# Moving the first weights of stage 3, and their high and low parts, into the last group of stages 0-2

## The chip, the cores and the metric

The kernel runs on one core of one Trainium2 chip. The time is the device time of one execution in microseconds (us); lower is better. The engines are named as the profile names them: PE is TensorE, DVE is VectorE, ACT is ScalarE, POOL is GpSimd, SP is SyncE.

## What is computed

The reference is a chain of four blocks over 16 batch entries of 128 rows and 256 columns, all in float32, with a context of the same shape:

```python
x = _L0_xattn_ref(x, ctx, ...)          # attention over channels, context as keys and values
x = _L1_xattn_ref(x, ctx, masks, ...)   # self-attention, cross-attention to ctx, MLP (tanh gelu)
x = _L2_xattn_ref(ctx, x, mask, ...)    # "lat": latents x attend to ctx and x, rms norm, MLP
# stage 3: two cross-attentions to ctx, 16 heads of width 128, then an MLP (exact gelu)
res = x; h = _layer_norm(x, ln1_scale, ln1_offset)
x = res + _cross_attention(h, ctx, wq1, bq1, wk1, bk1, wv1, bv1, wo1, bo1, bias_k1, bias_v1)
...
```

## The kernel before

The kernel has two blocks. `stages_0_to_2` computes the first three reference blocks, `stage_3` the fourth. A block ends with a meeting of all engines; no instruction of stage 3 starts before all of the block before has ended.

**Stages 0-2.** The 16 batch entries are taken as 8 groups (g = 0 to 7) of two. Each group passes through a layer of steps, and the steps of neighbouring groups are interleaved by a plan: `SCORES`, `WORK`, `NORMS`, `ADDS` and `MASKS` hold a due time for each step, a group's steps are due 100 plan units after those of the group before, and the sorted lists `TENSOR_ORDER`, `VECTOR_ORDER`, `SCALAR_ORDER` and `GPSIMD_ORDER` are the programs of the engines. All engines work their lists in order. In the last group nothing of a later group fills the gaps. Its end is a chain: the last attention (`lat`) gives `lat_o`; VectorE adds the residual (`residual`, line 713) and takes its statistics; `norm("rms", 7)` turns them into a factor through 13 steps on 128x2 elements, each waiting for the one before (lines 737 to 763), and scales two 128x256 rows (line 747); TensorE transposes them (line 821), ScalarE copies them out (line 564), TensorE runs the eight ups (line 834), ScalarE the gelus (line 598), TensorE the downs (line 855), and VectorE adds the residual to `X`.

**Stage 3.** TensorE multiplies in the format fp32r, with each operand kept as a high part (HI, a rounded copy) and a low part (LO, the original minus the high part); a product is three passes (`PASSES`, `split_matmul`, line 1789). High parts are casts on ScalarE (`split_hi`, line 1376; `context_high`, line 1495), low parts subtracts on GpSimd (`split_lo`, line 1265; line 1277) or VectorE (`context_low`, line 1700). SyncE loads the raw weights of the next pair of heads (`load_qk`, `load_v`, `load_o`). The attention runs over 2 x 8 pairs of heads, the middle ones in a loop (`pair`). Before the first pair there is an opening, the section "open": ScalarE and VectorE make the parts of `ctxT` and of the first weights, VectorE computes the norm of all 16 rows of X in `norm_factors` (lines 1621 to 1638) and half of the normalised rows (`xhat_rows`, line 1643), ScalarE the other half. TensorE's order in the opening is keys 4 and 5, values 0 (24 matmuls), transposes of rows 0 and 1 (16, line 1800), keys 6, values 1 and so on, into four PSUM banks that are used in turn (`OPEN_WORK`); VectorE's `copy_k` (line 1567) and `copy_v` (line 1574) empty them.

## Time and profile before

| what | value |
| --- | --- |
| time, median of 3 runs (lowest to highest) | 2135.85 us (2134.97 to 2145.02) |
| the profiled execution's own time | 2138.81 us |
| its span, first to last instruction | 2136.7 us |
| mean granted TensorE clock, as a share of full speed | 0.973 |
| TensorE busy | 1941.6 us, 91% of the span |
| VectorE, ScalarE, GpSimd busy | 1275.5, 1187.1, 671.9 us (60%, 56%, 31%) |
| seam between the two blocks | about 957 us after the start |

Busy time is an average over stages with different limits: what a change in one place is worth is read from that place. Times in a timeline are microseconds from the start of the span. Where several equal instructions are merged (x4), the time is that of all. What stands in square brackets is the idle time of the engine before them and what ended it. The granted clock is 1 at 2.4 GHz and 0.5 at 1.2 GHz.

### The profile page before, as it was taken

The page shows a single profiled execution, that of the slowest core. Times are in us where ns is not written, and L with a number is a line of the kernel's source. Part 1 is how long each engine was busy: PE and PEld are TensorE (multiplying, and loading weights), DVE is VectorE, ACT ScalarE, POOL GpSimd, SP SyncE. Part 2 cuts the span into 40 slices and gives each one's busy share as a digit, 9 for nine tenths or more (in the row PEclk, how much of TensorE's full clock was granted, in tenths as well). Part 3 has the DMA queues.
Part 4 walks back from the last instruction along what each step waited for, and adds up shares of the span by engine and source line. Part 5 has one row for each costly group of instructions (what it writes and reads, how often), then busy time and mean ns, then how long its engine had stood idle before and what let it go on. Part 6 is the DMA issues. An engine that isn't in the chain of part 4 may idle for free.

```text
span 2136.7 us, 43190 instructions
## 1 busy us (share of the span) xinstructions
PE 1941.6 (91%) x14880; PEld 1683.4 (79%) x14880; DVE 1275.5 (60%) x4128; ACT 1187.1 (56%) x3882; POOL 671.9 (31%) x611
## 2 busy tenths in 40 slices
PE   4678899999999989868999999999899999999889
PEld 3457678787777777647899999998789999999778
DVE  3577797978787765426455555556555555555663
ACT  2367877878787777425444444444544444444531
POOL 1233444444444443214222221223321222122462
PEclk8799999999999999968999999999999999999999
DMA  6000000000000000001000000000000000000100
GB/s 258 8 9 7 6 12 2 12 4 4 4 4 4 2 1 1 1 16 44 21 25 25 20 15 25 17 23 26 10 26 16 25 25 20 15 20 0 40 11 30
DMA packets 24635, 44.35 MB, mean 21 GB/s; under 512 B 2336, under 2 KB 12064, under 8 KB 23584
## 3 DMA queue, kind: packets, MB, share of 16 engines
q1 hardware_dynamic: 23040, 33.67, 5.1%
q10 hardware_dynamic: 1440, 8.72, 1.0%
q8 instruction: 85, 1.39, 0.3%
q14 instruction: 70, 0.57, 0.1%
HBM read 40.28 MB, written 2.10 MB: 20 GB/s over the span
## 4 chain that ended last, share of the span: by engine, by line
PE 49%; DVE 3%; ACT 2%; issue 1%; POOL 1%; ACTq 0%; DVEq 0%
PE general L1789 33%; PE o_psum L1844 6%; PE scores L1828 5%; PE pT_psum L1903 3%; PE scores L1954 1%; ACT probs L1411 1%; DVE oT L1599 1%; ACT oT L1427 1%; PE o_psum L1954 1%; PE pT_psum L1954 1%; POOL probs L1314 0%; PE general L1800 0%; DVE guess L1625 0%; DVE qT L1643 0%; ACT kT L1394 0%
## 5 line engine op out<-in xcount | busy, mean ns | idle before, releaser
L489 POOL TENSOR_TENSOR probs<-probs,rsums 128x512 f32<-128x512 f32 (+1 forms) x288 | 282.7, 994 | 507.8 <-DVE rsums L691 507.1
L1314 POOL TENSOR_TENSOR probs<-probs,rsums 128x512 f32<-128x512 f32 x128 | 133.2, 1040 | 743.3 <-DVE rsums L1592 743.3
L525 ACT ACTIVATE probs<-negated,negmax 128x128 f32<-128x128 f32 (+1 forms) x768 | 325.4, 431 | 12.4 <-DVE negmax L682 12.1
L964 PE MATMUL pT_psum<-ident,probs 128*128 128x128 f32 x1088 | 179.4, 287 | 60.1 <-ACT probsT L533 29.0
L1419 ACT COPY probsT<-pT_psum 128x512 f32<-128x512 f32 x128 | 74.9, 585 | 286.2 <-PE pT_psum L1903 286.2
L964 PEld LDWEIGHTS pT_psum<-ident,probs 128*128 128x128 f32 x1088 | 126.9, 145 | 117.5 <-issue 65.7
L1789 PE MATMUL general<-ctxT,w_qk 128*128 128x512 f32 x768 | 201.4, 398 | 12.2 <-POOL w_qk L1265 7.0
L1789 PE MATMUL general<-hT,w_qk 128*128 128x512 f32 x768 | 205.9, 403 | 1.5 <-POOL hT L1283 0.8
L1789 PE MATMUL general<-w_o,oT 128*128 128x256 f32 x1536 | 192.7, 280 | 13.7 <-DVE oT L1599 13.7
L1789 PEld LDWEIGHTS general<-w_o,oT 128*128 128x128 f32 x1536 | 185.3, 188 | 22.6 <-DVE oT L1599 19.0
L1411 ACT ACTIVATE probs<-scores,negmax 128x128 f32<-128x128 f32 x512 | 180.1, 370 | 23.8 <-DVE negmax L1584 23.7
L1427 ACT ACTIVATE oT<-o_psum,hcols 128x512 fp32r<-128x512 f32 x128 | 88.0, 687 | 184.9 <-PE o_psum L1844 184.9
L1789 PEld LDWEIGHTS general<-w_v,ctxT 128*128 128x128 f32 x1536 | 185.0, 188 | 4.8
L1789 PE MATMUL general<-w_v,ctxT 128*128 128x256 f32 x1536 | 187.0, 278 | 0.0
L1789 PEld LDWEIGHTS general<-ctxT,w_qk 128*128 128x128 f32 x768 | 144.1, 190 | 43.8 <-POOL w_qk L1265 7.4
L697 DVE COPY probsT<-pT_psum 128x512 f32<-128x512 f32 (+1 forms) x144 | 93.9, 652 | 129.6 <-PE pT_psum L964 129.6
L1599 DVE SCALAR_TENSOR_TENSOR oT<-o_psum,hcols,oT 128x512 fp32r<-128x512 f32 x128 | 96.1, 751 | 122.3 <-ACT oT L1427 122.3
L1789 PEld LDWEIGHTS general<-hT,w_qk 128*128 128x128 f32 x768 | 136.2, 189 | 25.5 <-POOL hT L1283 1.0
L834 PE MATMUL general<-hT_y,weights_a 128*128 128x256 f32 x640 | 153.4, 386 | 2.8 <-ACT hT_y L564 1.9
L533 ACT COPY probsT<-pT_psum 128x512 f32<-128x512 f32 (+1 forms) x144 | 80.3, 558 | 131.1 <-PE pT_psum L964 127.7
L525 ACT ACTIVATION_READ_ACCUMULATOR probs<-negated,negmax 128x1 f32 x768 | 148.8, 194 | 0.0
L1844 PE MATMUL o_psum<-probsT,ctxT 128*128 128x128 f32 x1024 | 141.8, 281 | 1.4 <-ACT probsT L1419 1.4
(182 smaller groups left out, 3897.6 us busy)
## 6 DMA issues: line engine op xcount, KB each, us to landing
raw_qk<-w_qk_dram SPq DMA_DIRECT2D x32, 256.0 KB, 2.8
weights_a<-weights_a_dram ACTq DMA_DIRECT2D x2, 2048.0 KB, 18.1
raw_v<-w_v_dram SPq DMA_DIRECT2D x16, 256.0 KB, 2.7
raw_vrows<-vrows_dram SPq DMA_DIRECT2D x16, 256.0 KB, 3.4
raw_o<-w_o_dram SPq DMA_DIRECT2D x16, 256.0 KB, 2.6
weights_a<-weights_a_dram ACTq DMA_DIRECT2D x3, 1024.0 KB, 10.2
X<-x_dram SPq DMA_DIRECT2D x8, 256.0 KB, 7.7
ctx_in<-ctx_dram SPq DMA_DIRECT2D x8, 256.0 KB, 3.0
```

Of the source, the lines that this page charges most:

```text
L489: nc.gpsimd.tensor_tensor(pr, pr, rsums[:, n % 4, 0:segs].unsqueeze(2).broadcast_to([P, segs, width(kind) // segs]), ALU.mult).then_inc(s[ ...
L525: last = nc.scalar.activation(probs[:, n % PROBS, i * wide:(i + 1) * wide], src[:, i * wide:(i + 1) * wide], ACT.Exp, scale=1.0 if kind == ...
L697: nc.vector.tensor_copy(probsT[:, n % 4, 0:width(kind)], pT_psum[:, 0:width(kind)]).then_inc(s["pT_copied_dve"], 1)
L834: last = nc.tensor.matmul(out[:, j * RA:(j + 1) * RA], w[weight][:, c, chunk * P:(chunk + 1) * P], rhs(c), start=(c == 0), stop=(c == KC - 1))
L964: last = nc.tensor.transpose(pT_psum[:, j * P:(j + 1) * P], probs[:, n % PROBS, j * P:(j + 1) * P], ident[:, :])
L1314: nc.gpsimd.tensor_tensor(pr, pr, rsums[:, t % 2, :].unsqueeze(2).broadcast_to([P, NB, P]), ALU.mult).then_inc(s["probs_ready"], 1)
L1411: nc.scalar.activation(probs[:, t % 2, b * P:(b + 1) * P], scores[t % 2][:, b * P:(b + 1) * P], ACT.Exp, bias=negmax[:, t % 2, b:b + 1], s ...
L1427: nc.scalar.activation(oT[:, HI, head, quarter(t % G)], o_psum[:, :], ACT.Identity, bias=hcols[:, bass.ds(at, 1)]).then_inc(s["o_hi"], 1)
L1599: nc.vector.scalar_tensor_tensor(out=oT[:, LO, head, quarter(t % G)], in0=o_psum[:, :], scalar=hcols[:, bass.ds(at, 1)], in1=oT[:, HI, hea ...
L1789: last = nc.tensor.matmul(out, stationary(a, c), moving(b, c), start=(i == 0), stop=(i == len(terms) - 1))
L1828: last = nc.tensor.matmul(scores[t % 2][:, j * P:(j + 1) * P], qT[:, head, b * P:(b + 1) * P], kT[:, head, b * P:(b + 1) * P], start=True, ...
L1844: last = nc.tensor.matmul(o_psum[:, j * P:(j + 1) * P], v[:, head, (t % G) * NB + j, :], probsT[:, j * P:(j + 1) * P], start=True, stop=True)
```

## The change

The raw weights of the first pair of stage 3 (`w_qk` for both heads, `w_v`, `vrows`, `w_o`), `hcols` and `rows` are loaded by SyncE in the last group of stages 0-2, after the last down projection of `mlp1` has been made. ScalarE makes the high parts of `w_qk`, `w_v` and the whole of `ctxT` (seven casts) before it reads the `rms` transposes of group 7; GpSimd makes the low parts, and `vrow`, after its last add (three subtracts of 128x512, one of 128x256, four of 128x1024). VectorE makes no part of `ctxT` any more. The buffers, of which `early_parts` fixes the addresses before both blocks, lie over tensors of stages 0-2 that are dead by then; for that `WEIGHTS_A` and the order of the allocations are changed, so that the weights of `lat` and `mlp2`, which are still in use, lie elsewhere. The loads' order in stages 0-2 is the same. In stage 3 the corresponding loads, casts and subtracts and the waits on them are gone, and the semaphores are made before both blocks. The diff, cut to its core (the reordered allocations, the semaphore list and unchanged context are left out):

```diff
-WEIGHTS_A = [("wq0", 1, P), ("wk0", 1, P), ("wv0", 1, P),
+WEIGHTS_A = [("lat_q", KC, D), ("lat_k", KC, D), ("lat_v", KC, D), ("lat_o", KC, D),
+             ("mlp2_up", KC, F), ("mlp2_down", FC, D),
+             ("wq0", 1, P), ("wk0", 1, P), ("wv0", 1, P),
              ("self_q", KC, D), ("self_k", KC, D), ("self_v", KC, D), ("self_o", KC, D),
              ("cross_k", KC, D), ("cross_v", KC, D), ("cross_q", KC, D), ("cross_o", KC, D),
-             ("mlp1_up", KC, F), ("mlp1_down", FC, D),
-             ("lat_q", KC, D), ("lat_k", KC, D), ("lat_v", KC, D), ("lat_o", KC, D),
-             ("mlp2_up", KC, F), ("mlp2_down", FC, D)]
+             ("mlp1_up", KC, F), ("mlp1_down", FC, D)]
+LAST_WEIGHTS = sum(k * n for name, k, n in WEIGHTS_A if name.startswith(("lat", "mlp2")))
...
         READERS = {"ln1": ("self_q", "self_k", "self_v"), "ln2": ("cross_q",), "ln3": [f"mlp1_up{i}" for i in range(4)],
                    "lat": ("lat_q", "lat_k", "lat_v"), "rms": [f"mlp2_up{i}" for i in range(4)]}
         ROW_OF = {"self": 0, "cross": 1, "mlp1": 2, "lat": 3, "mlp2": 4}
+        late = early["s"]
+        def early_splits():
+            w_qk, raw_qk = early["w_qk"], early["raw_qk"]
+            yield "raw_qk0_loaded", 16, w_qk[:, 0, HI, :], w_qk[:, 0, LO, :], raw_qk[:, 0, :], "qk0_ready"
+            yield "raw_v_loaded", 32, early["w_v"][:, HI, :], early["w_v"][:, LO, :], early["raw_v"][:, :], "wv_ready"
+            yield "raw_qk1_loaded", 16, w_qk[:, 1, HI, :], w_qk[:, 1, LO, :], raw_qk[:, 1, :], "qk1_ready"
         with nc.Block() as block:
                     else:
                         load_mask_lat(g)
+                wait_made(sp, "mlp1_down", GA - 1)
+                for head in range(2):
+                    sp.dma_start(early["raw_qk"][:, head, :], dram["w_qk"][0, :, head, :]).then_inc(late[f"raw_qk{head}_loaded"], 16)
+                sp.dma_start(early["raw_v"][:, :], dram["w_v"][0, :, :]).then_inc(late["raw_v_loaded"], 16)
+                sp.dma_start(early["raw_vrows"][:, :, :].rearrange("p j n -> p (j n)"), dram["vrows"][0, :].partition_broadcast(P)).then_inc(late["raw_v_loaded"], 16)
+                sp.dma_start(early["raw_o"][:, :], dram["w_o"][0, :, :]).then_inc(late["raw_o_loaded"], 16)
+                sp.dma_start(early["hcols"][:, :], dram["hcols"]).then_inc(late["vectors_loaded"], 16)
+                sp.dma_start(early["rows"][:, :, :], dram["rows_b"].partition_broadcast(P)).then_inc(late["vectors_loaded"], 16)
+                sp.wait_ge(late["vectors_loaded"], 32)
             @block.gpsimd
             def _(pool):
                 nc.gpsimd.memset(v_self[:, :, :], 0.0).then_inc(s["v_zeroed"], 1)
                         cross_mask(g)
                     else:
                         lat_mask(g)
+                for i, (_, _, high, low, raw, ready) in enumerate(early_splits()):
+                    pool.wait_ge(late["hi_done"], i + 1)
+                    nc.gpsimd.tensor_tensor(low, raw, high, ALU.subtract).then_inc(late[ready], 1)
+                nc.gpsimd.tensor_tensor(early["vrow"][:, :], early["raw_vrows"][:, 0, :], early["raw_vrows"][:, 1, :], ALU.subtract).then_inc(late["vrow_ready"], 1)
+                for i in range(B // NB):
+                    at = slice(i * R, (i + 1) * R)
+                    pool.wait_ge(late["ctxT_hi"], i + 1)
+                    nc.gpsimd.tensor_tensor(early["ctxT"][:, LO, :, at], ctxT[:, :, at], early["ctxT"][:, HI, :, at], ALU.subtract)
             @block.scalar
             def _(act):
                     elif "_up" in name:
                         gelus(name[:4], int(name[-1]), g)
+                def early_high_parts():
+                    wait_made(act, "mlp1_down", GA - 1)
+                    for loaded, count, high, _, raw, _ in early_splits():
+                        act.wait_ge(late[loaded], count)
+                        nc.scalar.copy(high, raw).then_inc(late["hi_done"], 1)
+                    for i in range(B // NB):
+                        at = slice(i * R, (i + 1) * R)
+                        nc.scalar.copy(early["ctxT"][:, HI, :, at], ctxT[:, :, at]).then_inc(late["ctxT_hi"], 1)
                 for piece, kind, g, u in SCALAR_ORDER:
+                    if (piece, kind, g) == ("read", "rms", GA - 1):
+                        early_high_parts()
                     if piece == "exps":
                         exps(kind, g, u)
                     elif piece == "copy_act":
...
-def stage_3(nc, dram, consts):
+EARLY_BUFFERS = {"ctxT": ([P, 2, KC, B * P], F32R), "raw_qk": ([P, 2, 2 * KC * P], F32), "raw_v": ([P, KC * 2 * P], F32), "raw_o": ([P, 2 * D], F32),
+                 "raw_vrows": ([P, 2, 2 * P], F32), "w_qk": ([P, 2, 2, 2 * KC * P], F32R), "w_v": ([P, 2, KC * 2 * P], F32R), "w_o": ([P, 2, 2 * D], F32R),
+                 "vrow": ([P, 2 * P], F32), "hcols": ([P, 2 * NH * HCOLS], F32), "rows": ([P, len(ROWS_B), D], F32)}
+EARLY_BYTES = sum(4 * int(np.prod(shape[1:])) for shape, _ in EARLY_BUFFERS.values())
+def early_parts(nc, ctx):
+    early = {}
+    with ExitStack() as reserved:
+        reserved.enter_context(nc.sbuf_tensor("reserved", [P, LAST_WEIGHTS], F32))
+        for name, (shape, dt) in EARLY_BUFFERS.items():
+            early[name] = reserved.enter_context(nc.sbuf_tensor(name + "3", shape, dt))
+    early["s"] = {n: ctx.enter_context(nc.semaphore(n + "3")) for n in (
+            "raw_qk0_loaded", "raw_qk1_loaded", "raw_v_loaded", "raw_o_loaded", "raw_up_loaded", "raw_down_loaded",
...
             return ctx.enter_context(nc.semaphore(name))
         X = consts["X"]
+        s = early["s"]
+        kT = sb("kT3", [P, 2, B * P])
+        xhat_last = sb("xhat3", [P, 2 * NB, D])
+        sb("early3", [P, EARLY_BYTES // 4])
+        ctxT, raw_qk, raw_v, raw_o, raw_vrows = [early[name] for name in ("ctxT", "raw_qk", "raw_v", "raw_o", "raw_vrows")]
+        w_qk, w_v, w_o, vrow, hcols, rows = [early[name] for name in ("w_qk", "w_v", "w_o", "vrow", "hcols", "rows")]
         hT = sb("hT3", [P, 2, KC, B * P], F32R)
-        ctxT = sb("ctxT3", [P, 2, KC, B * P], F32R)
         qT = sb("qT3", [P, 2, B * P])
-        kT = sb("kT3", [P, 2, B * P])
         raw_ctxT = consts["ctxT"]
         v = raw_ctxT[:, :, :].rearrange("p c r -> p (c r)").rearrange("p (h b k) -> p h b k", h=2, b=B)
         oT = sb("oT3", [P, 2, 2, B * P], F32R)
...
                 def load_o(pair):
                     sp.dma_start(raw_o[:, :], dram["w_o"][bass.ds(pair, 1), :, :].rearrange("a p n -> p (a n)")).then_inc(s["raw_o_loaded"], 16)
-                load_qk(0, 0)
-                load_qk(0, 1)
-                load_v(0)
-                load_o(0)
                 def next_weights(pair, following):
...
                     pool.wait_ge(s["raw_v_loaded"], loads)
                     nc.gpsimd.tensor_tensor(vrow[:, :], raw_vrows[:, 0, :], raw_vrows[:, 1, :], ALU.subtract).then_inc(s["vrow_ready"], 1)
-                split_lo(qk_parts(0), raw_qk[:, 0, :], 1, "qk0_ready")
-                value_rows(32)
-                split_lo(v_parts, raw_v[:, :], 2, "wv_ready")
-                for g in range(G // 2, G):
-                    pool.wait_ge(s["ctxT_hi"], g + 1)
-                    nc.gpsimd.tensor_tensor(ctxT[:, LO, :, quarter(g)], raw_ctxT[:, :, quarter(g)], ctxT[:, HI, :, quarter(g)], ALU.subtract).then_inc(s["ctxT_late"], 1)
-                split_lo(qk_parts(1), raw_qk[:, 1, :], 3, "qk1_ready")
                 def split_h(a, g):
...
             @block.scalar
             def _(act):
                 seed(act, [s["exp_done"], s["pT_copied"], s["o_hi"], s["hi_done"], s["xhat_act"], s["hT_hi"]])
-                act.dma_start(hcols[:, :], dram["hcols"]).then_inc(s["vectors_loaded"], 16)
-                act.dma_start(rows[:, :, :], dram["rows_b"].partition_broadcast(P)).then_inc(s["vectors_loaded"], 16)
                 def split_hi(name, loads, parts, raw):
...
                         xhat_rows(a + 1, 0)
                     copy_o(a, i, n, STEPS - 1)
-                def context_high(g):
-                    nc.scalar.copy(ctxT[:, HI, :, quarter(g)], raw_ctxT[:, :, quarter(g)]).then_inc(s["ctxT_hi"], 1)
-                context_high(0)
-                context_high(1)
-                split_hi("raw_qk0_loaded", 16, qk_parts(0), raw_qk[:, 0, :])
-                context_high(2)
-                split_hi("raw_v_loaded", 32, v_parts, raw_v[:, :])
-                context_high(3)
                 xhat_rows(0, 0)
-                split_hi("raw_qk1_loaded", 16, qk_parts(1), raw_qk[:, 1, :])
                 xhat_rows(0, 1)
-                act.wait_ge(s["vectors_loaded"], 32)
                 norm_copies("open", 0, 0, [0, 1])
                 norm_copies("open", 0, 1, [0, 1])
...
                     for half in range(2):
                         copy_v(section, 0, 0, t, half, section == "turn")
-                def context_low(g):
-                    dve.wait_ge(s["ctxT_hi"], g + 1)
-                    nc.vector.tensor_tensor(ctxT[:, LO, :, quarter(g)], raw_ctxT[:, :, quarter(g)], ctxT[:, HI, :, quarter(g)], ALU.subtract).then_inc(s["ctxT_ready"], 1)
-                context_low(0)
                 norm_factors(slice(0, B), B)
                 wait_step()
                 dve.wait_ge(s["norm_ready"], 2)
                 xhat_rows(0)
-                context_low(1)
                 xhat_rows(1)
-                dve.wait_ge(s["vectors_loaded"], 32)
                 copy_k("open", 0, 0, 4, 0, 0)
                 copy_k("open", 0, 0, 5, 0, 0)
-                dve.wait_ge(s["ctxT_ready"], G // 2 + 1)
-                dve.wait_ge(s["vrow_ready"], 2)
                 next_values("open", 0)
                 xhat_rows(2)
                 copy_k("open", 0, 0, 6, 0, 0)
                 next_values("open", 1)
                 xhat_rows(3)
                 copy_k("open", 0, 0, 7, 0, 0)
-                dve.wait_ge(s["ctxT_late"], 1)
                 next_values("open", 2)
                 norm_copy("open", 0, 2)
-                dve.wait_ge(s["ctxT_late"], 2)
                 next_values("open", 3)
                 norm_copy("open", 0, 3)
                 front(0, 0)
                                                 start=(f == 0 and k == 0), stop=(f == FC - 1 and k == len(PASSES) - 1))
                     return last
-                pe.wait_ge(s["qk0_ready"], 2)
-                pe.wait_ge(s["ctxT_ready"], 2)
                 keys("open", 0, 0, 4, 0)
-                pe.wait_ge(s["ctxT_ready"], 3)
                 keys("open", 0, 0, 5, 0)
-                pe.wait_ge(s["wv_ready"], 2)
                 next_values("open", 0)
                 transposed("open", 0, 0)
                 transposed("open", 0, 1)
-                pe.wait_ge(s["ctxT_late"], 2)
                 keys("open", 0, 0, 6, 0)
```

## Rows read from the trace of the kernel before

**Rows 1.** The page: the span.

```profile
span 2136.7 us, 43190 instructions
```

**Rows 2.** Timeline of TensorE: start, us, engine, line, op, out<-in, count [idle before <-releaser].

```profile
935.15 1.09 PE L821 MATMUL general<-ident,xhat_y 128*128 128x128 f32 x4 [5.36 <-DVE xhat_y L747]
937.16 10.05 PE L834 MATMUL general<-hT_y,weights_a 128*128 128x256 f32 x32 [0.93 <-ACT hT_y L564]
948.23 7.14 PE L855 MATMUL general<-weights_a,upT 128*128 128x256 f32 x32 [1.02 <-ACT upT L598]
962.38 2.92 PE L1789 MATMUL general<-ctxT,w_qk 128*128 128x512 f32 x6 [7.00 <-POOL w_qk L1265]
970.51 2.93 PE L1789 MATMUL general<-ctxT,w_qk 128*128 128x512 f32 x6 [5.20 <-DVE ctxT L1700]
...
976.29 1.91 PE L1800 MATMUL general<-ident,qT 128*128 128x128 f32 x16
```

**Rows 3.** Timeline of VectorE where stage 3 opens.

```profile
959.54 1.22 DVE L1700 TENSOR_TENSOR ctxT<-ctxT 128x1024 fp32r<-128x1024 f32 x1 [2.65 <-ACT ctxT L1495]
960.68 1.16 DVE L1621 BATCH_NORM_AGGREGATE mv<-row_stats 128x2 f32<-128x6 f32 x16
...
964.97 2.19 DVE L1643 TENSOR_SCALAR qT<-X,mv,rstd 128x256 f32<-128x256 f32 x2
967.09 3.37 DVE L1700 TENSOR_TENSOR ctxT<-ctxT 128x1024 fp32r<-128x1024 f32 x1
970.38 3.74 DVE L1643 TENSOR_SCALAR qT<-X,mv,rstd 128x256 f32<-128x256 f32 x2
974.04 1.52 DVE L1567 TENSOR_SCALAR kT<-general,hcols 128x512 f32<-128x512 f32 x2
975.48 0.68 DVE L1574 TENSOR_TENSOR ctxT<-general,vrow 128x512 f32<-128x512 f32 x1
...
977.10 0.73 DVE L1643 TENSOR_SCALAR xhat<-X,mv,rstd 128x256 f32<-128x256 f32 x2
```

**Rows 4.** Timeline of GpSimd where stage 3 opens.

```profile
961.05 1.27 POOL L1265 TENSOR_TENSOR w_qk<-raw_qk,w_qk 128x512 fp32r<-128x512 f32 x1 [40.95 <-ACT w_qk L1376]
...
965.70 1.32 POOL L1265 TENSOR_TENSOR w_v<-raw_v,w_v 128x512 fp32r<-128x512 f32 x1
966.97 5.71 POOL L1277 TENSOR_TENSOR ctxT<-ctxT 128x1024 fp32r<-128x1024 f32 x2
972.64 1.33 POOL L1265 TENSOR_TENSOR w_qk<-raw_qk,w_qk 128x512 fp32r<-128x512 f32 x1
```

**Rows 5.** Two source lines: count, duration in ns min/median/max, first and last start.

```profile
L737 DVE TENSOR_TENSOR newton<-mv x8: 161/966/970, 312.0 to 931.8; 128x2 f32<-128x2 f32 x8
...
L739 DVE SCALAR_TENSOR_TENSOR var<-mv,newton x8: 160/161/161, 313.0 to 932.0; 128x2 f32<-128x2 f32 x8
```

**Rows 6.** Timeline of ScalarE in the last group and at the seam.

```profile
925.86 0.37 ACT L549 ACTIVATE oT_y<-o_psum,cols 128x128 f32<-128x128 f32 x1 [4.06 <-PE o_psum L994]
936.27 0.84 ACT L564 ACTIVATE hT_y<-general,cols 128x256 f32<-128x256 f32 x2 [10.04 <-PE general L821]
...
958.47 1.99 ACT L1495 CAST ctxT<-ctxT 128x1024 fp32r<-128x1024 f32 x2 [10.38 <-issue]
960.36 0.61 ACT L1376 CAST w_qk<-raw_qk 128x512 fp32r<-128x512 f32 x1
```

**Rows 7.** Timeline of VectorE in the norm of the last group.

```profile
931.82 0.16 DVE L737 TENSOR_TENSOR newton<-mv 128x2 f32<-128x2 f32 x1
...
932.42 0.17 DVE L755 TENSOR_SCALAR guess<-guess 128x2 int32<-128x2 int32 x1
```

**Rows 8.** Table by window: us, busy of each engine, granted clock, DMA share.

```profile
960.00:961.00 1.00, 0.00 (x0) 0.00 (x0) 1.00 (x6) 1.00 (x3) 0.00 (x0) 0.55 0.90 213
...
942.00:944.00 2.00, 2.00 (x8) 1.69 (x7) 0.00 (x0) 0.20 (x1) 0.00 (x0) 0.74 0.00 0
...
973.00:974.00 1.00, 1.00 (x7) 0.90 (x6) 1.00 (x1) 0.00 (x0) 0.97 (x1) 0.63 0.00 0
```

## Prediction of the time after the change

> **What bounds the kernel now.** The page first: TensorE is the engine that the span follows, so the places where it stands still are what a change can give back. I looked for those around the seam between stages 0-2 and stage 3, since the change touches nothing else: the span is 2136.7 us [rows 1]. The timeline of TensorE around the seam says where the idle time sits [rows 2]. The last down projection ends at 955.37 (948.23 + 7.14). The first keys start at 962.38, 7.00 us later, released by GpSimd's low part of `w_qk`. The second keys start at 970.51 after another 5.20 us, released by VectorE's low part of `ctxT`. From there TensorE runs with hardly a gap: 24 value matmuls, the 16 transposes of the normalised rows at 976.29, and on through the first scores.
>
> Why the second wait is so long is in VectorE's and GpSimd's timelines, read side by side [rows 3, 4]. A 128x1024 subtract took VectorE 1.22 us at 959.54 and 3.37 us at 967.09; the two normalised rows at 964.97 took 2.19 us, the next two at 970.38 took 3.74, where the two at 977.10, beside an idle GpSimd, cost 0.73. GpSimd in that stretch ran `w_v` low (965.70 to 967.02), two `ctxT` lows (966.97 to 972.68, the first about 2.4, the second about 3.3 us) and `w_qk` low (972.64 to 973.97). Laid over each other they alternate: VectorE's second row waits for the end of `w_v`, its subtract for the end of the first `ctxT` low, the second `ctxT` low for the end of VectorE's subtract, VectorE's next row for the end of that, and its last for the end of `w_qk`. So the two engines hold something in common, whole instruction by whole instruction, in turn. The same is seen with tiny operands: the 128x2 multiply of line 737 takes 161 ns alone and up to 970 ns, with a median of 966, where GpSimd is normalising [rows 5].
>
> **Part 1: what the opening of stage 3 loses, and the time it gives back.** Removed there: 2 DMA issues on ScalarE, 5 on SyncE, 4 ScalarE casts of `ctxT`, 3 of weights, 2 VectorE and 2 GpSimd lows of `ctxT`, 3 GpSimd lows of weights and the `vrow` subtract, with the waits of TensorE and VectorE on them. What is late next is VectorE's norm chain and the copies behind it. VectorE ended stage 2 at 956.89 (959.54 - 2.65) and ScalarE did its first work of stage 3 at 958.47 after two DMA issues [rows 3, 6]; I take 958.3 for VectorE's first instruction, bounds 957.5 and 959.5. Then, from [rows 3]: aggregates to shift took 960.68 to 964.97, 4.3 us, less about 0.3 of a wait for `w_qk` low that is gone: 962.3. Four normalised rows without GpSimd: 2 x 0.73 = 1.4, at 963.7. Two key copies, 1.52: 965.2. Two value copies of 0.68: 966.6. ScalarE's half of the normalised rows runs beside it. TensorE needs two keys of 6 matmuls and 24 value matmuls with twice the columns of a key. A key took 2.93 us at 1.2 GHz [rows 2, 8], so 1.5 at 2.4, and the values 3.0: 964.3, or 965.7 with the first key at the lower clock. Its 16 transposes go bank by bank behind VectorE's copies: the first four when keys 4 are copied at 964.5, the last four at 966.6, done at 967.1. Before, they were done at 978.2 (976.29 + 1.91). All that follows up to the first score is TensorE work with nothing else late: its inputs (high parts on ScalarE, GpSimd's `split_h`) move with the transposes. So the first score comes 978.2 - 967.1 = **11.1 us** earlier measured from the seam, 10.9 with 0.2 for the handing over of banks. Bounds: 9.4 (low clock through both keys, 1.5 us more) and 11.7 (VectorE ready at 957.5). SyncE's loads for the second pair find their buffers free at once and nobody waits for them.
>
> **Part 2: what the last group gains in work.** SyncE issues 7 DMAs behind its last mask load; it has nothing else queued, they are gated by the last `mlp1_down`, which the order of work (`WORK`) puts 120 plan units ahead of the last `lat_o`. Before the change the first of the same loads had landed, been cast and been used within 9 us of the seam (`w_v` low at 965.70 [rows 4]). Cost nothing, covered by the attention of the last group between. ScalarE is idle from 926.23 to 936.27, 10.04 us, before it reads `rms` of group 7 [rows 6]. Into that hole go 3 casts of 0.61 and 4 of 1.0 (1.99 for two), less overlap: 5.8 us, done by 932. Behind them waits only the `rms` copy at 936.27, so they cost nothing as long as the hole is over 6 us; without it they would cost those 6.
>
> GpSimd is idle from 920.10 (961.05 - 40.95) [rows 4] and now gets: `w_qk` low from 926.8 (0.08 behind ScalarE's cast) 1.27, `w_v` 1.32, `w_qk` 1.3, `vrow` 0.7 (an estimate: half the elements of `w_v`), so 931.4; then four `ctxT` lows of 2.4 each, back to back: 9.6 us. Nothing reads them before stage 3 at 957, so GpSimd's own time is free. But beside them lies the one chain that TensorE waits for there: VectorE's `rms` norm. After the residual and its stats it runs, from 931.82, 13 tiny steps of 0.2 us, each waiting for the one before, and two 128x256 rows [rows 7]; TensorE starts at 935.15, when they end, and after it comes the whole last MLP [rows 2]. With the turn-taking of [rows 3, 4]: step 1 (line 737) waits for the first `ctxT` low, to 933.9; the second low, queued meanwhile, goes next, and step 2 waits to 936.5; step 3 to 938.9, step 4 (line 755) to 941.6. Then GpSimd is empty. Line 755 ended at 932.59 before: **9.0 us later**, and the rest of the chain, TensorE, the MLP and the end of stage 2 shift with it. Nothing hides this: TensorE has no other work there (5.4 us idle before 935.15), and the table load and ups sit behind the norm. If the two int32 steps (lines 753 and 755) don't take turns, steps 5 and 6 do in their place: 941.6 against 932.98 (0.56 behind the start of line 755), 8.6 us. If the residual or its stats took turns too, they would only use up turns counted here: GpSimd's queue ends at the same time, within the 0.2 us that a turn adds.
>
> Nothing in the trace shows 13 tiny VectorE steps against a full GpSimd queue, so I bound the term: nothing (no turn missed), 1.9 us (one wait, to 933.75, then VectorE keeps the way), 9.0 (a turn each time). I take 9.0, since in [rows 3, 4] five hand-overs out of five go to the engine that was already waiting.
>
> The Trainium skill, "SBUF — State Buffer", Who interferes with whom, has a rule against this change: a VectorE instruction with two SBUF inputs, or in a two-port mode, and a GpSimd instruction exclude each other for a whole instruction, the one that starts first going first. It does not say who is next when both are queued; by it the sum could be the 1.9 or the 9.0. "VectorE: DVE Perf Modes" counts one-source SBUF instructions among those that may use both ports, whatever the type, which would put the int32 steps in and give 9.0 rather than 8.6; no row here shows an int32 step beside GpSimd.
>
> **The sum.** -10.9 + 9.0 = -1.9 us. The profiled execution took 2138.81 us around a span of 2136.7; it would become 2136.9. The median of the three runs shown is 2.96 us below the profiled one, so the forecast is 2135.85 - 1.9 = **2134.0 us**. The parts' bounds give 9.4 to 11.7 of gain and 8.6 to 9.0 of loss: -3.1 to -0.4. TensorE's clock widens that. In the last MLP TensorE ran at 1.2 GHz until about 943 (mean granted 0.74 in 942 to 944) [rows 8], 8 us after its transposes; in the opening it was at 1.2 GHz only from 970.51 to about 973.7. With a short stretch like that in the last MLP, some 2 us less. So -5 to +1 for this case, 2131 to 2137.
>
> **The rivals.**
> A, the tiny steps slip through: VectorE waits once, 1.9 us, or not at all. For it: in the steps of line 737 only the first is stretched, the next one (line 739, at most 161 ns) never is [rows 5]; but there GpSimd's queue had run dry. Then -9.0 to -10.9, 2125 to 2127, and only its far end, with a lucky clock, passes 0.5%.
> B, slower: the clock. TensorE now stands still 14.4 us instead of 5.4 before the last ups. The 32 downs took 7.14 us, 0.22 each, at 2.4 GHz, so 0.45 at 1.2; the 32 ups took 10.05, a part of them at the lower clock [rows 2]. If all of them run there they take 14.3, 4.2 us more, and with 1.5 us in the opening the sum is -1.9 + 5.7 = +3.8, 2139.7. It turns the sign from 9 more matmuls at 1.2 GHz on (1.9 / 0.22). Against it: TensorE had already fallen to 1.2 GHz before 935.15, so the longer rest adds nothing to start from. The clock fell at about 960, 4.7 us after TensorE stopped [rows 8], and in the new opening it rests some 3 us, so it may not fall at all there.
> C, the change does not open earlier: something else, hidden so far, holds TensorE until 965 or so, for example code behind the block boundary. ScalarE's start at 958.47 speaks against it. From 965 TensorE's keys and values take 6.0 us and the transposes 0.9 (at least half of their 1.91), so they are done at 971.9, 6.3 us earlier than before instead of 10.9: +2.7 in all, 2138.6.
>
> **How the numbers follow.** The forecast case 0.75, A 0.13, B 0.07, C 0.05. The range takes the bounds of the forecast case, A down to 2125 and nearly all of B and C: 2125 to 2139. A measurement of this kernel can tell about 0.5%, 10.7 us, from no change. Faster by over that: only the far end of A, 0.05. Slower by over that: none of the cases, 0.02 for what I don't see. Within it 0.93.
>
> **What would show it.** In the profile of the changed kernel: TensorE's first keys some 3 us after the last down matmul with no wait on GpSimd or VectorE, and the transposes done some 12 us after the last down matmul instead of 22.8; ScalarE's seven casts inside its idle stretch; GpSimd with four 128x1024 subtracts of 2.4 us, and lines 737 to 755 of the norm of group 7 at 2 us each instead of 0.16, TensorE's wait before the last `rms` transposes 14 us instead of 5.4. The prediction is wrong if those steps stay at 0.16 us or only the first is stretched (A), if the clock in the last ups stays at half throughout (B), or if the opening still holds a wait over 3 us (C).

## The result, with the profile after

The changed kernel takes 2146.28 us (median of 9 executions, 2143.41 to 2151.73), the kernel before, run in turn with it, 2136.45 us (median of 9, 2130.55 to 2145.02). The ratio is 1.005, with a 95% interval of 1.0037 to 1.0062: 9.8 us slower, where 1.9 us faster was forecast. The time lies above the forecast range of 2125 to 2139 us.

The page of the changed kernel, first its span and then the busy time of each engine (us, share of the span, instructions):

```profile
span 2141.6 us, 43183 instructions
PE 1947.6 (91%) x14880; PEld 1693.5 (79%) x14880; DVE 1270.5 (59%) x4126; ACT 1187.8 (55%) x3882; POOL 675.5 (32%) x613
```

The profiled execution took 2143.41 us. TensorE is busy 6 us longer than before (1941.6), though the change gives it no matmul. To see where, the span is cut at two events that both kernels have: the last `lat_o` and the first score of stage 3. TensorE's timeline around the seam, where start, duration, line, operation and count are followed by the idle time before it:

```profile
922.21 3.47 PE L892 MATMUL general<-weights_a,oT_y 128*128 128x256 f32 x8 [0.48 <-ACT oT_y L585]
938.95 1.09 PE L870 MATMUL general<-ident,xhat_y 128*128 128x128 f32 x4 [13.26 <-DVE xhat_y L796]
940.97 9.50 PE L883 MATMUL general<-hT_y,weights_a 128*128 128x256 f32 x32 [0.93 <-ACT hT_y L600]
951.49 7.14 PE L904 MATMUL general<-weights_a,upT 128*128 128x256 f32 x32 [1.02 <-ACT upT L634]
961.53 4.37 PE L1812 MATMUL general<-ctxT,w_qk 128*128 128x512 f32 x12 [2.89 <-DVEq L197]
965.69 3.27 PE L1812 MATMUL general<-w_v,ctxT 128*128 128x256 f32 x24
968.80 1.91 PE L1823 MATMUL general<-ident,qT 128*128 128x128 f32 x16
986.44 1.06 PE L1851 MATMUL scores<-kT,qT 128*128 128x128 f32 x8
```

The wait before the last `rms` transposes is 13.26 us [rows 2: 5.36]. The two waits at the start of stage 3 [rows 2: 7.00 and 5.20] have become one of 2.89, and the transposes are done 12.1 us after the last down matmul (970.71 less 958.63) instead of 22.8. From `lat_o` to the first score it takes 64.23 us; in the trace of before it is 67.54, from these two rows of TensorE's timeline:

```profile
926.28 3.50 PE L843 MATMUL general<-weights_a,oT_y 128*128 128x256 f32 x8 [0.48 <-ACT oT_y L549]
...
993.82 1.06 PE L1828 MATMUL scores<-kT,qT 128*128 128x128 f32 x8
```

So the seam is 3.3 us shorter in these two traces, and the loss lies elsewhere.

What made the 13.26 us is in VectorE's timeline over the same stretch:

```profile
927.73 1.77 DVE L786 TENSOR_TENSOR newton<-mv 128x2 f32<-128x2 f32 x1
929.53 2.26 DVE L788 SCALAR_TENSOR_TENSOR var<-mv,newton 128x2 f32<-128x2 f32 x1
931.82 2.27 DVE L802 TENSOR_SCALAR guess<-var 128x2 int32<-128x2 int32 x1
934.13 2.27 DVE L804 TENSOR_SCALAR guess<-guess 128x2 int32<-128x2 int32 x1
936.43 0.16 DVE L808 SCALAR_TENSOR_TENSOR newton<-guess 128x2 f32<-128x2 f32 x1
```

beside it in GpSimd's:

```profile
926.44 0.74 POOL L533 TENSOR_TENSOR vrow<-raw_vrows 128x256 f32<-128x256 f32 x1
927.12 9.24 POOL L537 TENSOR_TENSOR ctxT<-ctxT 128x1024 fp32r<-128x1024 f32 x4
```

and in ScalarE's:

```profile
923.61 3.88 ACT L666 CAST ctxT<-ctxT 128x1024 fp32r<-128x1024 f32 x4
940.07 0.84 ACT L600 ACTIVATE hT_y<-general,cols 128x256 f32<-128x256 f32 x2 [12.58 <-PE general L870]
```

Four steps on two elements per partition take 8.57 us together, 0.16 each before [rows 7], and each ends with one of GpSimd's four subtracts of 2.3 us. The fifth, with GpSimd's queue empty from 936.36, is back at 0.16. ScalarE's seven casts, three of weights and four of `ctxT`, run from 922.06 to 927.49; it is then idle for another 12.58 us, so they cost nothing.

Outside the seam, the stretch from the first score to the end of TensorE's last matmul is 1152.16 us, and 1139.82 in the trace of before: 12.3 us longer, in code that the diff does not touch. The groups of matmuls by line from 1000 to 2130 us (count | busy us, mean ns of one | idle before), of the kernel before:

```profile
L1789 PE MATMUL general<-w_o,oT 128*128 128x256 f32 x1536 | 192.7, 280 | 13.7 <-DVE oT L1599 13.7
L1789 PE MATMUL general<-ctxT,w_qk 128*128 128x512 f32 x738 | 190.9, 394 | 0.0
L1789 PE MATMUL general<-w_v,ctxT 128*128 128x256 f32 x1440 | 174.8, 277 | 0.0
L1789 PE MATMUL general<-hT,w_qk 128*128 128x512 f32 x744 | 199.6, 403 | 1.5 <-POOL hT L1283 0.8 <-ACT kT L1394 0.7
```

and of the changed one:

```profile
L1812 PE MATMUL general<-w_o,oT 128*128 128x256 f32 x1536 | 200.4, 285 | 13.7 <-DVE oT L1634 13.7
L1812 PE MATMUL general<-ctxT,w_qk 128*128 128x512 f32 x732 | 187.9, 392 | 0.0
L1812 PE MATMUL general<-w_v,ctxT 128*128 128x256 f32 x1440 | 182.3, 283 | 0.0
L1812 PE MATMUL general<-hT,w_qk 128*128 128x512 f32 x732 | 196.1, 403 | 1.5 <-POOL hT L1331 0.8 <-ACT kT L1440 0.7
```

The same number of matmuls on `w_o` takes 7.7 us more, those on `w_v` 7.5 us more, with idle time before them unchanged. In the timeline of the middle pairs one group of 24 matmuls takes 2.91 us before and 3.04 after; first a row of the kernel before, then one of the changed kernel:

```profile
1185.72 2.91 PE L1789 MATMUL general<-w_v,ctxT 128*128 128x256 f32 x24
```

```profile
1180.38 3.04 PE L1812 MATMUL general<-w_v,ctxT 128*128 128x256 f32 x24
```

There are 64 groups on `w_v` and 64 on `w_o` in the kernel. 128 x 0.13 would be 16.6 us, but not every group is of the shortest kind, and the rows above give 15.2. The keys (`ctxT,w_qk`) take 392 ns each instead of 394, some 1.5 us less over their 768 matmuls; the queries (`hT,w_qk`) stay at 403. An account without overlaps comes from the starts of the matmuls in the two traces, each one's start to the next one's, up to TensorE's last `o_psum` group of the attention: the products on `w_v` take 7.1 us more and those on `w_o` 7.2, the keys 1.6 less and the queries 0.3 less. That is 12.4 us, the whole difference of that stretch (1036.04 and 1023.64 us from the first score).

What the change did to those matmuls is to put their operands elsewhere. The addresses, in bytes from the start of a partition, that the allocation gives:

| tensor | before | after | before, modulo 128 | after, modulo 128 |
| --- | --- | --- | --- | --- |
| `w_qk` | 196096 | 118080 | 0 | 64 |
| `w_v` | 204288 | 126272 | 0 | 64 |
| `w_o` | 208384 | 130368 | 0 | 64 |
| `hT` | 50496 | 139072 | 64 | 64 |
| `ctxT` | 83264 | 75072 | 64 | 64 |
| `oT` | 148800 | 188224 | 64 | 64 |

In `split_matmul` on `w_v` one operand is `ctxT`, on `w_o` one is `oT`. So weights and activations started 64 bytes apart modulo 128 before, and start alike after.

### The profile page after: what moved, and what is told of

It is laid out like the page before. It is cut to its first block, busy times and chain, and to the rows that moved or that the text cites. A ratio compares the mean times of both kernels' runs of the same rounds, so it can differ in the third digit from the quotient of the medians.

```text
span 2141.6 us, 43183 instructions
## 1 busy us (share of the span) xinstructions
PE 1947.6 (91%) x14880; PEld 1693.5 (79%) x14880; DVE 1270.5 (59%) x4126; ACT 1187.8 (55%) x3882; POOL 675.5 (32%) x613
## 4 chain that ended last, share of the span: by engine, by line
PE 49%; DVE 2%; ACT 2%; issue 1%; POOL 1%; ACTq 0%; DVEq 0%
PE general L1812 33%; PE o_psum L1867 6%; PE scores L1851 5%; PE pT_psum L1926 3%; PE scores L1977 1%; ACT probs L1457 1%; DVE oT L1634 1%; ACT oT L1473 1%; PE pT_psum L1977 1%; PE o_psum L1977 1%; POOL probs L1362 0%; PE general L1823 0%; DVE guess L1660 0%; ACT kT L1440 0%; ACT xhat L1430 0%
## 5 line engine op out<-in xcount | busy, mean ns | idle before, releaser
L1812 PE MATMUL general<-w_o,oT 128*128 128x256 f32 x1536 | 200.4, 285 | 13.7 <-DVE oT L1634 13.7
L1812 PEld LDWEIGHTS general<-w_o,oT 128*128 128x128 f32 x1536 | 192.4, 192 | 22.3 <-DVE oT L1634 19.0
L1812 PEld LDWEIGHTS general<-w_v,ctxT 128*128 128x128 f32 x1536 | 192.3, 192 | 4.5
L1812 PE MATMUL general<-w_v,ctxT 128*128 128x256 f32 x1536 | 194.8, 283 | 0.0
```

The lines of the kernel that those rows point to most:

```text
L1812: last = nc.tensor.matmul(out, stationary(a, c), moving(b, c), start=(i == 0), stop=(i == len(terms) - 1))
```

## The experiments

The theory at this point: 12 us are lost because of where the operands lie, and the seam does what the prediction said (10.6 to 10.9 us gained in the opening, 8 to 9 lost to the turns of GpSimd and VectorE). The rivals: the longer groups come from other work that the change put beside them, or from a lower clock outside the seam; and in the seam, the wait of 13.26 us is a late load and not turn-taking. "Seam" below is the time from the last `lat_o` to the first score, "rest" from there to TensorE's last matmul, each from one trace of the kernel. A time of a whole kernel is a median.

### Moving buffers and nothing else

The changed kernel with the weights on multiples of 128, `a1_after_w_on_128` (`hT`, `qT` and `oT` move along by 128):

```diff
-                 "raw_vrows": ([P, 2, 2 * P], F32), "w_qk": ([P, 2, 2, 2 * KC * P], F32R), "w_v": ([P, 2, KC * 2 * P], F32R), "w_o": ([P, 2, 2 * D], F32R),
+                 "raw_vrows": ([P, 2, 2 * P], F32), "pad_a": ([P, 16], F32), "w_qk": ([P, 2, 2, 2 * KC * P], F32R), "w_v": ([P, 2, KC * 2 * P], F32R), "w_o": ([P, 2, 2 * D], F32R), "pad_b": ([P, 16], F32),
```

> The changed kernel with two 64-byte pads, so that w_qk, w_v and w_o of stage 3 start at multiples of 128 bytes again (118144, 126336, 130432), as they did before the change; all other addresses keep their remainder. Theory P (the start address modulo 128 of w_v and w_o sets the rate of the matmuls that read them): a group of 24 matmuls on w_v or w_o in the loop falls from 3.04 us back to 2.91, the 6 of a key or query go from 1.52 back to 1.54, and the time falls by some 12 us, to about 2134, a little under the kernel before. Theory D (where in SBUF the buffers lie, by kilobytes): 3.04 stays and the time stays at 2146. Theory T (the matmuls are slower since stage 3 begins at another moment or beside other transfers): 3.04 stays.

Measured: 2140.55 us against 2135.42 of before (ratio 1.0015, 1.000 to 1.003). The groups on `w_o` went back to 2.90 us, those on `w_v` only to 2.99; the rest is 1146.62, some 5.5 us better than in the changed kernel. So places matter, but "a multiple of 128" is not all of it.

The kernel before with its weights 64 bytes past a multiple of 128, `a2_before_w_off_128`:

```diff
+        sb("pad_a", [P, 16])
         w_qk = sb("w_qk3", [P, 2, 2, 2 * KC * P], F32R)
...
+        sb("pad_b", [P, 16])
         raw_vrows = sb("raw_vrows3", [P, 2, 2 * P])
```

> The kernel before with two 64-byte pads, so that w_qk, w_v and w_o start 64 bytes past a multiple of 128; nothing else changes. Theory P: 24 matmuls on w_v or w_o take 3.04 us instead of 2.91, the 6 of a key 1.52 instead of 1.54, and the time rises by some 12 us to 2148. Theories D and T: no change, 2136.

Measured: 2144.99 us (1.005, 1.0036 to 1.0064), rest 1152.63. Its groups by line, same stretch as above:

```profile
L1791 PE MATMUL general<-w_o,oT 128*128 128x256 f32 x1536 | 201.7, 287 | 13.7 <-DVE oT L1601 13.7
L1791 PE MATMUL general<-w_v,ctxT 128*128 128x256 f32 x1440 | 182.3, 283 | 0.0
```

Sixty-four bytes ahead of the weights make the kernel before as slow as the changed one, with the same rows. The program is otherwise the same instruction by instruction, so other work beside the matmuls is not left as a cause. Nor is the clock: its mean granted share was 0.976 in this trace and 0.977 in that of the changed kernel, where it was 0.973 before, and between 1000 and 2000 us it was 1.00 in all three.

The kernel before with the activations moved to multiples of 128 too, `a4_before_all_on_128`:

```diff
+        sb("pad_0", [P, 16])
         hT = sb("hT3", [P, 2, KC, B * P], F32R)
...
+        sb("pad_a", [P, 16])
         w_qk = sb("w_qk3", [P, 2, 2, 2 * KC * P], F32R)
```

> The kernel before with every matmul operand of stage 3 at a multiple of 128 bytes: hT, ctxT, qT, kT, oT, which all start 64 bytes past one, move by 64, and the weights stay on one. Theory P in its wide form (any moving operand off the 128 bytes is slow): the keys and queries, whose moving operands are ctxT and hT, get faster than 1.54 us for 6, by about 0.02 to 0.07, 256 groups of them, and the time falls by 5 to 18 us. In its narrow form (only the relation between stationary and moving start counts, fast when they differ by 64): the groups on w_v and w_o get slower, 3.04, and the time rises by 10 or more. Theories D and T: no change.

Measured: 2146.45 us (1.0055, 1.0036 to 1.0074), groups of 3.04, rest 1152.13. Everything on multiples of 128 is as slow as everything 64 past them: what counts is how the two operands stand to each other, not how each stands.

### The turns in the last group

The changed kernel, with GpSimd held before its four `ctxT` subtracts until VectorE has made the normalised rows of the last group, `a3_after_lows_behind_norm`:

```diff
+                wait_xhat(pool, "rms", GA - 1)
                 for i in range(B // NB):
```

> The changed kernel, where GpSimd waits for the normalised rows of the last rms before its four low parts of ctxT. If turn-taking of GpSimd and VectorE is what holds the rms chain, lines 737 to 755 of the kernel before go back from about 2.2 us each to 0.16, TensorE's wait before the last rms transposes falls from 13.3 us to under 6, and the time falls by 8 to 9 us against the changed kernel, to about 2138. If the casts on ScalarE or something else holds that chain, the wait stays over 10 us and the time at 2146. The 3.04 us groups of w_v and w_o stay in every theory.

Measured: 2137.04 us (1.0011, 1.0001 to 1.0021), 9.2 us under the changed kernel. The seam is 56.93 us, 7.3 less than in the changed kernel, and the rest 1149.87. TensorE's timeline:

```profile
926.20 3.58 PE L893 MATMUL general<-weights_a,oT_y 128*128 128x256 f32 x8 [0.48 <-ACT oT_y L586]
935.14 1.09 PE L871 MATMUL general<-ident,xhat_y 128*128 128x128 f32 x4 [5.37 <-DVE xhat_y L797]
958.39 2.97 PE L1813 MATMUL general<-ctxT,w_qk 128*128 128x512 f32 x12 [2.98 <-DVEq L197]
983.13 1.06 PE L1852 MATMUL scores<-kT,qT 128*128 128x128 f32 x8
```

VectorE's, its first two tiny steps:

```profile
931.82 0.16 DVE L787 TENSOR_TENSOR newton<-mv 128x2 f32<-128x2 f32 x1
932.02 0.16 DVE L789 SCALAR_TENSOR_TENSOR var<-mv,newton 128x2 f32<-128x2 f32 x1
```

and GpSimd's:

```profile
935.08 9.26 POOL L538 TENSOR_TENSOR ctxT<-ctxT 128x1024 fp32r<-128x1024 f32 x4 [3.93 <-DVE xhat_y L797]
```

The wait before the transposes is 5.37 again and the steps are 0.16, while all loads, casts and other subtracts are where the change put them. So the whole of the added wait was turn-taking. The subtracts end at 944.34, 14 us ahead of their first reader: moved behind the norm they cost nothing. The seam is 10.6 us shorter than before (67.54 less 56.93), which is what the opening gives back with the turns taken out, measured against this one trace of the kernel before.

Against other traces it gives back less. The padded forms of the kernel before run the same instructions there, and in `a2`, `a4` and `c3` (the last is described below) TensorE's second wait is 1.61, 1.59 and 3.09 us instead of 5.20, the transposes are done 19.2, 19.4 and 21.1 us after the last down matmul instead of 22.8, and the seam is 63.33, 64.28 and 64.88 us instead of 67.54. In `a2` VectorE's second `ctxT` subtract took 1.22 us, where it took 3.37 [rows 3]:

```profile
962.46 1.22 DVE L1702 TENSOR_TENSOR ctxT<-ctxT 128x1024 fp32r<-128x1024 f32 x1
962.53 1.73 POOL L1271 TENSOR_TENSOR vrow<-raw_vrows 128x256 f32<-128x256 f32 x1 [3.39 <-DMA raw_vrows<-vrows_dram]
963.73 2.93 PE L1791 MATMUL general<-ctxT,w_qk 128*128 128x512 f32 x6 [1.61 <-DVE ctxT L1702]
```

GpSimd's `vrow` step, which waits for a load, starts 10.3, 10.1 and 9.8 us after the last down matmul in `a2`, `a4` and `c3`, and 9.6 in the trace of before. In these four traces, the later it comes, the more of VectorE's work is ahead of it and the shorter the opening; nothing was tried to bring this about. With the transposes done 12.0 us after the last down matmul in `a3`, the opening gives back 7 to 11 us, and the changed kernel's seam of 64.23 us is anything from 3.3 us shorter to 0.9 longer. Where the kernel before lies in most executions, no run shows.

### Which distance

The next four keep `a3`'s wait and move `w_v` and `w_o` by 192, 64, 320 and 448 bytes with `w_qk` left in place, and `hT`, `qT`, `oT` by 512 (s is 48, 16, 80 and 112 floats):

```diff
-                 "raw_vrows": ([P, 2, 2 * P], F32), "w_qk": ([P, 2, 2, 2 * KC * P], F32R), "w_v": ([P, 2, KC * 2 * P], F32R), "w_o": ([P, 2, 2 * D], F32R),
+                 "raw_vrows": ([P, 2, 2 * P], F32), "w_qk": ([P, 2, 2, 2 * KC * P], F32R), "pad_a": ([P, s], F32), "w_v": ([P, 2, KC * 2 * P], F32R), "w_o": ([P, 2, 2 * D], F32R), "pad_b": ([P, 128 - s], F32),
```

> The changed kernel with GpSimd's ctxT lows behind the norm (as in a3) and pads that move w_v and w_o by 192 bytes and hT, qT and oT by 512; w_qk stays. Of their 256-column products the start of the moving operand then lies 192 bytes past the start of the stationary one (ctxT, oT), modulo 512, as in the kernel before; in a3 the distance was 0. Theory R (what counts is the distance between the starts of the stationary and the moving operand, not the start of either): 24 matmuls on w_v and on w_o take 2.91 us, while the keys, whose distance stays 0, keep their faster 1.52 for 6. The 128 groups give back 0.13 each, 16.6 us: about 2120.5, 16 us under the kernel before. If only the absolute start modulo 128 of w_v counted, a1 would have had 2.91 on w_v and not 2.99, so that theory expects something between and no clear number.

Measured: 2132.75 us against 2136.88 (0.9979, 0.9966 to 0.9993), groups of 2.99 on both weights (a dozen on `w_v` of 2.90), not the 2.91 that was looked for, rest 1143.86. Its groups by line lie between the two kernels':

```profile
L1813 PE MATMUL general<-w_o,oT 128*128 128x256 f32 x1536 | 195.4, 282 | 13.7 <-DVE oT L1635 13.7
L1813 PE MATMUL general<-w_v,ctxT 128*128 128x256 f32 x1440 | 178.6, 281 | 0.0
```

> As b1, with w_v and w_o moved by 64 bytes (distance 64 modulo 512). Theory R: as w_v in a1, whose distance was 64, 24 matmuls take 2.99 us, on w_v and on w_o; about 2131. A theory in which the distance counts modulo 128 only expects 2.91 on both.

Measured: 2137.88 us (one execution), groups of 2.99, rest 1150.29.

> As b1, with w_v and w_o moved by 320 bytes (distance 320 modulo 512; 64 modulo 256). If the distance counts modulo 256, this is like 64: 2.99 us. If modulo 512, it is a value of its own, between 2.90 and 3.04.

Measured: 2134.64 us (one execution), groups of 2.99, rest 1149.46.

> As b1, with w_v and w_o moved by 448 bytes (distance 448, or -64, modulo 512). Theory R: as w_o in a1, whose distance was 448 modulo 512, 24 matmuls take 2.90 us, on both; about 2120.

Measured: 2139.01 us (one execution), 2.99 with a dozen groups on `w_v` at 2.90, rest 1146.95. The theory of a distance modulo 512 between a group's own two operands falls: in `a1` the distance from `oT` to `w_o` is the same as here, 57920 bytes, and its groups take 2.90, here 2.99. So does the theory of that distance modulo 128 alone, which looked for 2.91 in `b2`. What all the moves have in common so far: with equal starts modulo 128 the group takes 3.04, with different ones 2.90 or 2.99.

### What makes 2.99 into 2.91

`c2_w_all_apart_192` is `b1` with `w_qk` moved by the same 192 bytes, so that only the place of `w_qk` differs:

```diff
-                 "raw_vrows": ([P, 2, 2 * P], F32), "w_qk": ([P, 2, 2, 2 * KC * P], F32R), "pad_a": ([P, 48], F32), "w_v": ([P, 2, KC * 2 * P], F32R), "w_o": ([P, 2, 2 * D], F32R), "pad_b": ([P, 80], F32),
+                 "raw_vrows": ([P, 2, 2 * P], F32), "pad_a": ([P, 48], F32), "w_qk": ([P, 2, 2, 2 * KC * P], F32R), "w_v": ([P, 2, KC * 2 * P], F32R), "w_o": ([P, 2, 2 * D], F32R), "pad_b": ([P, 80], F32),
```

> As b1, but w_qk moves by 192 bytes too, together with w_v and w_o; hT, qT and oT stay where b1 has them (320 modulo 4096). If the pitch of the value matmuls in b1 (117 ns) was that of a neighbouring product whose operands lay wrong, w_v falls to 113 ns here (2.91 for 24), as in c1; if hT and oT have to lie right modulo 4096 too, w_o stays at 2.99. About 2126 in the one case, 2130 in the other.

Measured: 2126.62 us (one execution), groups of 2.91, rest 1142.35.

`c3_before_wqk_off_128` is the kernel before with `w_qk` moved by 64 bytes and `w_v`, `w_o` by 128:

```diff
+        sb("pad_a", [P, 16])
         w_qk = sb("w_qk3", [P, 2, 2, 2 * KC * P], F32R)
+        sb("pad_b", [P, 16])
         w_v = sb("w_v3", [P, 2, KC * 2 * P], F32R)
```

> The kernel before with w_qk alone moved by 64 bytes (64 past a multiple of 128, like ctxT and hT) and w_v, w_o by 128. Each product counted by itself: the keys get faster (1.52 for 6), w_v and w_o stay at 2.91: about 2132. If the products next to each other matter: w_v goes to 2.99 as in b1, and the time is about 2140.

Measured: 2138.08 us (one execution; before beside it 2136.27), groups of 2.99, rest 1146.18 against 1139.82. So in `b1` and `c2` a group on `w_v` or `w_o` takes 2.99 or 2.91 according to where `w_qk` lies, which that group does not read; the products next to it in TensorE's order do. `c3` points the same way, but there `w_v` and `w_o` have moved by 128 bytes as well. The remainder of `w_qk` modulo 128 alone does not decide it: it is 0 in `a1`, and the groups on `w_v` take 2.99 there. The pitch from one matmul's start to the next tells the same: in the kernel before it is 117 to 118 ns for the first four, and 113 from the sixth on; in `b1`, `b2`, `b3` and `c3` 117 to 120 all the way, nearly always 117 or 118; in the changed kernel 120. Why a neighbour's address should hold on through 24 matmuls is not settled.

### The changed kernel, placed as the kernel before

`c1_placed_as_before` has `a3`'s wait and two pads that put `w_qk`, `w_v`, `w_o`, `hT`, `ctxT`, `qT`, `kT` and `oT` at the same address modulo 4096 as in the kernel before:

```diff
-                 "raw_vrows": ([P, 2, 2 * P], F32), "w_qk": ([P, 2, 2, 2 * KC * P], F32R), "w_v": ([P, 2, KC * 2 * P], F32R), "w_o": ([P, 2, 2 * D], F32R),
+                 "raw_vrows": ([P, 2, 2 * P], F32), "pad_a": ([P, 48], F32), "w_qk": ([P, 2, 2, 2 * KC * P], F32R), "w_v": ([P, 2, KC * 2 * P], F32R), "w_o": ([P, 2, 2 * D], F32R), "pad_b": ([P, 336], F32),
...
+                wait_xhat(pool, "rms", GA - 1)
```

> The changed kernel with the ctxT lows behind the norm (as in a3) and pads that put all matmul operands of stage 3 at the same address modulo 4096 as in the kernel before: w_qk, w_v and w_o at 3584, hT, ctxT, qT, kT and oT at 1344. Theory R (the relation of the addresses of stationary and moving operand, including those of the products just before, sets the pitch): 24 matmuls on w_v and w_o take 2.91 us as in the kernel before (pitch 113 ns), the keys 1.54; the time is that of the kernel before less the 10.7 us that a3's trace gains up to the first score: about 2126. If something coarser than 4 KB counts, the pitch stays at 117 ns (2.99), about 2132.

Measured: 2123.74 us (2119.59 to 2127.41) against 2136.27: 0.9949, 0.9932 to 0.9966, faster than both kernels. Seam 56.31, rest 1139.78, that of before to 0.1 us. Its groups by line:

```profile
L1813 PE MATMUL general<-w_o,oT 128*128 128x256 f32 x1536 | 193.3, 280 | 13.7 <-DVE oT L1635 13.7
L1813 PE MATMUL general<-w_v,ctxT 128*128 128x256 f32 x1440 | 174.9, 278 | 0.0
```

`c4_after_placed_as_before` is the changed kernel with those two pads alone, so the change as the prediction took it: the work moved, the places kept.

> The changed kernel with the placement of c1 and nothing else: GpSimd's ctxT lows are again in front of VectorE's norm, as the change has them. This is the change without its side effect on the matmuls of stage 3. If placement and turn-taking are all there is, 24 matmuls on w_v and w_o take 2.91 us, TensorE waits some 13 us before the last rms transposes, and the time is that of c1 (2123.7) plus the 8.5 us of turn-taking: about 2132, 2 to 4 us under the kernel before (2136), which is what the prediction's sum said of the seam. If the change loses something else in stage 3, the time is 2136 or more. The difference of this run to the changed kernel (2146.3) is then the price of the placement, 12 to 14 us.

Measured: 2133.98 us against 2134.80 (ratio 0.9997, 0.9985 to 1.0009; 12 and 17 executions). The wait before the transposes is there, and the groups on `w_v` and `w_o` are short:

```profile
939.33 1.08 PE L870 MATMUL general<-ident,xhat_y 128*128 128x128 f32 x4 [13.26 <-DVE xhat_y L796]
...
1178.55 2.91 PE L1812 MATMUL general<-w_v,ctxT 128*128 128x256 f32 x24
1215.03 2.91 PE L1812 MATMUL general<-w_o,oT 128*128 128x256 f32 x24
```

The changed kernel less `c4` is 2146.28 - 2133.98 = 12.3 us, the price of the places. Each against the kernel before that ran in turn with it, the one is 9.8 us slower and the other 0.8 faster, which makes 10.6, and from the first score to the last `o_psum` group of the attention the two traces differ by 11.8 us (1036.04 and 1024.24). `c4` less `c1` is 10.2 us, the price of the turns by the time of the whole kernel (11.7 when each is taken against its own kernel before), where the seams of the two traces differ by 7.5 (63.82 and 56.31). The other 3.3 us of the traces lie in the rest (1143.08 against 1139.78), and 2.7 of them in the last MLP, 1000 us after the turns: it takes 118.84 us in `c4` and 116.18 in `c1`. Its last group of `scores` shows the clock: 7.47 us at a mean granted clock of 0.61 in the first 4 us in `c4`, 5.98 us at 1.00 in `c1`. The trace of the kernel before has the 7.47 too. So these 3 us are a difference between executions for the most part, and not a price of the turns.

## Why the prediction was wrong, point by point

**The step that failed** stands in its first paragraph: the places to look at are those around the seam, "since the change touches nothing else". The sum of part 1 and part 2 costs everything outside the seam at nothing, and names no work that would make it so. But the diff gives every operand of the split products of stage 3 a new address. With that, 128 groups of 24 matmuls take 3.04 us instead of 2.91, and the kernel is 11 to 12 us slower. No rival was about this; 0.02 was left for what was not seen. The runs show it in both directions: pads alone make the kernel before slower by 0.5% (`a2`, `a4`), and pads alone bring the changed one back to 0.9997 of it (`c4`). No row of the trace of before could have given the price, since all its operands lie in one place; but 91% of the span is matmul time, 787 us of it in the products with `w_qk`, `w_v` and `w_o`, which the diff moves, and such a term needed a bound of its own. The Trainium skill, "TensorE: Matmul & The Clock Gate", Part 2: What happens when you issue a matmul, says that loading the next weights takes no read bandwidth from the running matmul, since the two have ports of their own. That gives no reason for addresses to matter, and in `a2` they do, with 3.04 for 2.91 us. Whether the two reads collide or something else makes the difference, no run here shows, so the runs neither confirm nor refute the sentence.

**Part 1, the opening**: right in mechanism, and its size close with some luck. Forecast a gain of 10.9 us, measured 10.6 in the seam of `a3`, where the turns are out. But both numbers are taken from the same trace of the kernel before, whose opening is the longest of four; by the time from the last down matmul to the last transpose it is 10.8 us from that trace and 7.2 to 9.1 from the other three (19.2 to 21.1 less 12.0), under the lower bound of 9.4. The bounds allowed for the clock and for VectorE's start, and none for how the turns of the old opening fall. First keys 2.9 us after the last down, transposes done 12.1 us after it (in `a3` 967.40 less 955.41, 12.0), as forecast 3 and 12. One detail was off: the clock did fall in the changed kernel's opening. The windows there, whose columns are the stretch, its length, busy time of PE, PEld, DVE, ACT and POOL, granted clock, DMA share and GB/s:

```profile
961.50:963.00 1.50, 1.47 (x6) 1.30 (x7) 1.12 (x16) 0.00 (x0) 0.00 (x0) 0.93 0.65 208
963.00:965.00 2.00, 2.00 (x6) 1.52 (x6) 1.66 (x11) 0.00 (x0) 0.00 (x0) 0.50 0.71 229
```

Two keys took 4.37 us there, 2.97 in `a3`; that is nearly the 1.5 us that the bound of part 1 named. The transposes still end at the forecast time: in `a3` TensorE waited 0.60 us for VectorE's copy before them and a little again between them, and in the changed kernel the slower keys took up that slack.

**Part 2, ScalarE and SyncE at nothing**: right. Seven casts from 922.06 to 927.49, with 12.58 us of idle time behind them, and no wait on a load in the rows of TensorE or ScalarE in the seam.

**Part 2, the turns**: right in mechanism, and mis-sized by a little. Four steps took turns and the two int32 steps were among them. Forecast 9.0 us, found 7.9 (from `lat_o` to the transposes 16.74 us, before 8.87). The subtracts took 2.3 us, not 2.4, and the first of them was under way when step 1 came, which then waited 1.77. The wait is 13.26, where 14.4 was forecast. The Trainium skill, "SBUF — State Buffer", Who interferes with whom, makes such a pair exclude each other for a whole instruction; these rows agree, with 2.27 us for a step of 0.16.

**The sum for the seam**: -1.9 forecast, -3.3 between the two traces, +0.9 to -0.7 against the three padded ones, all inside its bounds of -5 to +1. With the places kept (`c4`) the kernel takes 2133.98 us, where 2134.0 was forecast for the change; the distance to before, -0.8 us, is inside the bounds and smaller than the interval, so such closeness is partly luck.

**The rivals**: A fell, since four steps were stretched and not one. B fell: the last ups took 9.50 us, before 10.05. C fell, with the first keys 2.9 us after the last down. The kernel did come out slower, but not by B, the rival on that side.

## What to carry to other kernels

A change that moves buffers changes every instruction that reads them: compare the duration of a repeated group of matmuls far away from the edit, and if it differs while its idle time does not, pad the buffers back to the old addresses before judging the rest of the change. Measure a move of work with the places held fixed, and one of the places with the work held fixed. Work put on GpSimd beside a chain of tiny VectorE steps cost one whole GpSimd instruction for each of four steps, until its queue was empty; one wait that puts it behind the chain was worth 8 to 12 us by the times of the whole kernel, 7.3 and 7.5 by the seams. And a gain that is worked out from one trace of a stretch where two engines take turns needs a second trace of it: the same opening lost between 1.6 and 5.2 us in its second wait.

## What the runs showed of the hardware

- The time of a group of 24 fp32r matmuls of 128x256 depends on where its operands lie: 3.04 us when both start alike modulo 128 bytes (the changed kernel, `a2`, `a3`, `a4`), 2.90 to 2.91 or 2.99 when they don't. With nothing else changed that is 0.5% of this kernel (`a2`).
- Between 2.91 and 2.99 the address of a tensor that only neighbouring products read can decide (`b1` and `c2`). The rule behind both is open; a start-to-start pitch of 113, 118 or 120 ns is all that the traces tell.
- The keys of six matmuls of 128x512 went the other way, 1.52 to 1.53 against 1.53 to 1.54 us (392 and 394 ns for one matmul), where the groups on `w_v` and `w_o` took 3.04. The queries stayed at 403 ns.
- VectorE and GpSimd went on in strict turns four times out of four when both had work queued (the changed kernel, `a1`, `c4`), and an int32 step with one input, 128x2, was held as long as a float32 step with two.
